# Loading the attention stacks of a group with six loads instead of seven, parts interleaved row by row

## The reference

```
q = layernorm(x) @ Wq;  k, v = split(ctx @ Wkv)        # 32 heads of 16
q, k = rope(q, pos), rope(k, pos)
x = x + softmax(q k^T / 4) v @ Wout + bout
h = gelu(bitlinear(layernorm(x), w_fc))                # 512 -> 2048
x = x + bitlinear(h, w_proj)                           # 2048 -> 512
```

## Time and profile before

| | us |
|---|---|
| median of 3 runs | 797.15 |
| the runs | 799.24, 793.47, 797.15 |
| the profiled execution | 797.79 |
| its span | 795.9 |
| busy: TensorE | 768.5 (97%) |
| busy: VectorE | 674.4 (85%) |
| busy: ScalarE | 456.1 (57%) |
| busy: GpSimd | 341.0 (43%) |

### The profile page before, as it was taken

The page is one execution under the profiler, slowest core; times in us unless marked ns, Lnnn a source line. Parts: engine busy times, 40 slices in busy tenths (PEclk is TensorE's granted clock), DMA queues, the critical chain, the costliest instruction groups (busy, mean ns, idle before and its releaser), DMA issues.

```text
span 795.9 us, 11662 instructions
## 1 busy us (share of the span) xinstructions
PE 768.5 (97%) x3812; PEld 331.6 (42%) x3812; DVE 674.4 (85%) x945; ACT 456.1 (57%) x811; POOL 341.0 (43%) x445
## 2 busy tenths in 40 slices
PE   4899999799999999999999999999999999999998
PEld 3688877233333222323322222244444444444443
DVE  7788998688888888888888888269999999898895
ACT  5677776477777777767777777734322333223430
POOL 4688777743454455445445544623222121110001
PEclk9999999699999999999999999999999999999999
DMA  8488897535577769796887996326456654555545
GB/s 288 127 216 241 256 254 184 129 109 137 147 141 152 154 158 142 152 171 149 146 155 180 171 176 137 82 57 137 107 110 144 132 106 93 108 117 87 112 87 137
DMA packets 178861, 117.22 MB, mean 147 GB/s; under 512 B 119746, under 2 KB 150514, under 8 KB 178802
## 3 DMA queue, kind: packets, MB, share of 16 engines
q1 hardware_dynamic: 178802, 116.49, 65.7%
HBM read 64.50 MB, written 25.43 MB: 113 GB/s over the span
## 4 chain that ended last, share of the span: by engine, by line
PE 86%; DMA 6%; DVE 3%; SPq 2%; POOL 1%; issue 1%; ACT 1%; POOLq 0%; ACTq 0%
PE banks L967 14%; PE banks L952 14%; PE banks L706 13%; PE banks L692 12%; PE banks L281 11%; PE banks L667 11%; PE banks L938 7%; DMA stack_words<-max_rows 4%; DMA max_rows<-max_parts 2%; PE banks L310 2%; SPq L584 1%; PE banks L678 1%; DVE maxima L740 1%; DMA attn_words<-in_x_dram 1%; ACT probs_words L760 1%
## 5 line engine op out<-in xcount | busy, mean ns | idle before, releaser
L760 ACT ACTIVATE probs_words<-banks 128x512 f32<-128x512 f32 x512 | 272.1, 598 | 101.7 <-PE banks L692 101.0
L740 DVE TENSOR_REDUCE maxima<-banks 128x2 f32<-128x1024 f32 x240 | 283.4, 1216 | 45.6 <-PE banks L667 45.5
L692 PE MATMUL banks<-stack_words 98*128 98x512 bf16 x512 | 175.4, 386 | 4.8 <-DMA stack_words<-max_rows 3.4
L667 PE MATMUL banks<-stack_words 96*128 96x512 bf16 x480 | 144.9, 383 | 0.0
L706 PE MATMUL banks<-probs_words,late_words 128*32 128x512 f32 x1024 | 137.3, 608 | 0.7
L952 PE MATMUL banks<-ternary_words,late_words 128*128 128x512 f16 x512 | 113.1, 380 | 0.0
L967 PE MATMUL banks<-ternary_words,stack_words 128*128 128x512 f16 x512 | 112.9, 380 | 0.0
L1130 ACT ACTIVATE probs_words<-probs_words,h_moments 128x2048 f32<-128x2048 f32 (+1 forms) x17 | 32.2, 1901 | 135.4 <-DVE h_moments L1027 135.4
L692 PEld LDWEIGHTS banks<-stack_words 98*128 98x128 bf16 x512 | 39.8, 98 | 150.0 <-ACT probs_words L760 109.9
L771 POOL TENSOR_SCALAR neg_max<-maxima 128x16 f32<-128x16 f32 x32 | 8.3, 258 | 163.0 <-DVE maxima L740 161.2
L967 PEld LDWEIGHTS banks<-ternary_words,stack_words 128*128 128x128 f16 x512 | 49.9, 98 | 64.4 <-issue 6.6
(11 more groups left out here) (139 smaller groups left out, 962.5 us busy)
## 6 DMA issues: line engine op xcount, KB each, us to landing
o_rows<-late_words SPq DMA_DIRECT2D x32, 256.0 KB, 3.3
k_parts<-ternary_words SPq DMA_DIRECT2D x48, 128.0 KB, 3.2
q_parts<-ternary_words SPq DMA_DIRECT2D x48, 128.0 KB, 2.5
stack_words<-q_parts SPq DMA_DIRECT2D x32, 192.0 KB, 3.1
stack_words<-k_parts SPq DMA_DIRECT2D x96, 64.0 KB, 2.7
stack_words<-k_parts SPq DMA_DIRECT2D x32, 192.0 KB, 2.7
attn_words<-in_x_dram SPq DMA_DIRECT2D x16, 256.0 KB, 4.4
probs_words<-in_L_ffn_w_fc_dram SPq DMA_DIRECT2D x16, 256.0 KB, 3.7
```

Of the source, the lines that this page charges most:

```text
L667: mm = self.nc.tensor.matmul(self.score_slot[j % 2][:, i], self.mem.q_stack[0:STACK, slot, head, c * P:(c + 1) * P], self.mem.k_stack[0:ST ...
L692: self.nc.tensor.matmul(self.st_bank[(g * 16 + k) % self.ST_BANKS], self.mem.k_stack[0:STACK + 2, slot, head, c * P:(c + 1) * P], self.mem ...
L740: dve.tensor_reduce(self.maxima[:, g % 2, 2 * j:2 * j + 2], self.score_slot[j % 2], AX.X, ALU.max).then_inc(self.scores_read, 1)
L760: act.activation(self.probs[:, c, head, :], self.st_bank[(g * 16 + k) % self.ST_BANKS], ACT.Exp, scale=1 / math.sqrt(HEAD)).then_inc(self. ...
```

## The change

`load_stacks` views the parts as (value) x (part) x (head, column): 16 rows in the outer dimension, the parts within. A load of several parts writes partition after partition in that order, so a stack's block of 48 partitions holds value 0 of parts 0, 1, 2, then value 1 of parts 0, 1, 2, and so on. `k_stack` gets in each such block one part of k repeated: part 0 three times, part 1 twice, part 2 once, by a source view that repeats the part. The pairs are the same six: q's parts 0, 1, 2 with k's part 0, q's 0, 1 with k's 1, and q's 0 with k's 2. There are six loads, q and k in turn, of 192, 192, 128, 128, 64 and 64 KB, 768 KB as before. Their place in SP's list is the same. `STACK_LOADS` follows.

```diff
-STACK_LOADS = DMA * 7
+STACK_LOADS = DMA * 6
...
-        for stack_sb, where, runs in (
-            (mem.q_stack, mem.q_parts, ((0, 0, 3), (3, 0, 2), (5, 0, 1))),
-            (mem.k_stack, mem.k_parts, ((0, 1, 1), (1, 0, 1), (2, 0, 1), (3, 0, 3))),
-        ):
-            src = where[g].rearrange("t (d h) c -> (t d) (h c)", h=GH)
-            for to, part, count in runs:
-                sp.dma_start(stack_sb[to * HEAD:(to + count) * HEAD, slot].rearrange("p h c -> p (h c)"),
-                             src[part * HEAD:(part + count) * HEAD]).then_inc(self.stacks_loaded[slot], DMA)
+        q_rows, k_rows = [where[g].rearrange("t (d h) c -> d t (h c)", h=GH) for where in (mem.q_parts, mem.k_parts)]
+        for part, to, count in ((0, 0, 3), (1, 3, 2), (2, 5, 1)):
+            at = slice(to * HEAD, (to + count) * HEAD)
+            sp.dma_start(mem.q_stack[at, slot].rearrange("p h c -> p (h c)"), q_rows[:, 0:count]
+                         ).then_inc(self.stacks_loaded[slot], DMA)
+            sp.dma_start(mem.k_stack[at, slot].rearrange("p h c -> p (h c)"),
+                         k_rows[:, part:part + 1].to_broadcast([HEAD, count, GH * SEQ])
+                         ).then_inc(self.stacks_loaded[slot], DMA)
```

## The result

The changed kernel takes 798.76 us in the median (796.05 to 805.09, 20 runs), the kernel before 797.28 us (793.47 to 799.24, 20 runs). The ratio is 1.0036 with a 95% interval of 1.0021 to 1.0050: 0.36%, 2.9 us, slower.

A forecast was written before the change was run, and what follows sets the result against it. TensorE was taken as the bound, its loop stalls hanging on the row maxima's load. Issue +0.5 and transfer 0 on the median 797.15 gave 797.7 us, set at 797.4 for a small gain; range near 791.5 to near 802.

The forecast's parts named there:

- the slack that I had read: Attention loop: in a group without a backlog the row maxima's load L596 has at least 1.2 us to spare.
- The bound: Attention loop: of TensorE's 3.44 us idle, 3.4 us in 6 waits is for the 8 KB row maxima load, L596.
- The issue term: SP's issue of the stack loads: six take 3.43 us, 0.17 longer than seven before.
- The transfer term: DMA engines carrying the 768 KB of stacks: taken as 0, with 1.3 us either way as the ends.
- What it costs: Attention loop: only the 6 groups with a TensorE wait pay 0.17 us each, +1.0 us, half taken: +0.5 us.
- The rule on joining small transfers: DMA queue: one load fewer would give 0.6 us a group, up to 3.4 us over six late groups; sum had 0.
- A: Rival: one load fewer on SP and in the queue ends the 6 maxima waits, 793.7 us, half 795.4; chance 0.24.
- B: Rival: the new source form is slow to carry, queue 1.3 us a group later, 807 us; chance 0.11.
- C: Rival: loads leave SP as seven would, with the same durations, 797.15 us within the runs' spread; chance 0.02.

The follow-up runs named there:

- runs with one plain side: Changed kernel with only q's, or only k's, three loads as plain consecutive rows (wrong pairing of parts): 1.0037, 799.30 us with plain q; 1.0022, 798.29 us with plain k.
- six plain loads: Order and number of the change's loads, but all of plain consecutive rows (other scores), against the kernel before: 0.9993, 796.16 us.
- nine loads: Kernel before with q's and k's loads of 48 rows each cut into 32 and 16, same rows and bytes: 1.0093, 803.77 us.

## Why the prediction was right or wrong

The class was right (within 1%), the sign too, and the time lies in the range; the size was not. I had +0.25 us on the median; the ratio says +2.9. That the class came out right is in part luck: two terms were too small, and the slack that I had read hid most of it. Of the signs that I named, six issues in a group with a sum of 3.61 us, L596 at 4.88, a period of 11.35 us in most groups and no wait of the score product came true; TensorE's wait of at most 5 us (it is 6.3 in this profile) and the queue's share near 51% (55 to 63%) did not. Step by step:

**The bound.** Right. The only stall that hangs on the loads is TensorE's wait for L596. It grew from 3.4 to 6.3 us, in a profile 5.8 us above its kernel's median. In the runs above it went roughly with the lateness of that load: 0.9 us with L596 at 4.10, 1.1 and 3.4 with 4.57, 3.1 to 3.5 with 4.67 to 5.03, 7.0 with 5.49.

**The issue term.** Right in sign, mis-sized: 0.17 us predicted, 4.88 - 4.58 = 0.30 measured. I took 0.575 us from the row of a source with a repeated dimension, and the loads with several parts took 0.58 to 0.63. What I missed is that q's load of 16 rows, plain in my sum with 0.42, took 0.58 too. The runs with one plain side show the cause: the issue behind a load of this form is also longer.

**The transfer term.** This is the step that failed. I took 0, with 1.3 us at the far end. Measured is an arrival 1.2 us later, of which 0.9 us is landing (2.7 to 3.6 us). The reason I gave, 64 KB and 192 KB landing in the same 2.7 us, was weak, since the profile does not measure loads of one semaphore apart, and it did not carry over to another order and number of loads. It was not the source form, as I had thought possible, but the rest: q and k in turn give about 0.6 us of arrival, six loads in place of seven 0.3 (7.7 us, with the issue 0.47 us shorter), the form 0.3 by its issue.

**What it costs.** I let only the 6 groups that had a wait pay, once each, and half of that. Who pays was right: calm groups take the whole 1.2 us out of their slack and wait for nothing (8 KB at 8.0 to 8.7 us, wanted at 8.99). What each late group pays was too low. In groups with a late transpose the 8 KB land 0.35 us later in the middle case (9.14 to 9.49), and 7 groups wait in place of 6. Seven to nine groups at 0.35 us are 2.5 to 3.2 us by my estimate, the size of the 2.9 measured.

**The rule on joining small transfers** ("DMA: Bandwidth & Descriptors" of the Trainium skill, section Rules for kernel authors), by which I had estimated 0.6 us a group for one load fewer, did not show in the time: with six plain loads it stayed (0.9993; the interval reaches 2.0 us down, not 3.4), and the bytes came later, not sooner. TensorE's waits did fall in that profile, from 3.4 to 0.9 us. The table of that page of the Trainium skill, from which the 0.6 us came, is of transfers that GpSimd issues to 128 partitions, which these are not.

**The rivals.** A did not occur: no wait went away. B had the mechanism, bytes that arrive late and a point at 1.2 us a group, and the wrong cause and price; the arrival stood just at that point, and the time 2.9 us up and not 10. C is ruled out by the timeline.

## What to carry to other kernels

Look for the small transfer that the critical engine waits for, and count what is issued and what is queued ahead of it: here 8 KB behind 768 KB. Fewer DMA issues are not less issue time when their sources get another dimension; and the price of lateness is paid where the small transfer is already late for another reason: 1.2 us of delay made no calm group wait, and 0.35 us in the late ones is about the size of the whole loss. Issuing the small transfer ahead of the last of the big ones gave more (0.3%) than any form of the big ones, as long as these still landed in time; moving big loads ahead of the small one's own producer gave nothing or harm.

## What the runs showed of the hardware

In the profiled run of the changed kernel at 804.57 us TensorE waited 2.36 us at 161.39 (and 1.94 us at 478.23), and then ran slow, which the profiled run of before does not do from 158 us on. Both runs have a slow stretch ahead of that, at the start of the loop, and in the changed kernel it ended earlier: from 150 to 158 us the clock was granted at 0.97, before at 0.61. L592 of group 1 starts at nearly the same time in both, 155.41 and 155.80. So TensorE, further on in the changed kernel, came to the maxima of group 1 before they were there. The lines are before, then after; the granted clock is third from the right:

```profile
150.00:158.00 8.00, 8.00 (x31) 1.99 (x29) 4.74 (x5) 4.53 (x9) 7.66 (x6) 0.61 0.36 56
150.00:158.00 8.00, 8.00 (x46) 2.22 (x44) 6.51 (x7) 5.74 (x11) 7.66 (x7) 0.97 0.53 57
```

The windows around the wait, of the changed kernel:

```profile
158.00:160.00 2.00, 1.04 (x8) 0.31 (x4) 1.52 (x2) 1.09 (x2) 0.05 (x1) 1.00 0.01 1
160.00:162.00 2.00, 0.61 (x2) 0.33 (x3) 0.30 (x1) 0.00 (x0) 1.36 (x4) 0.69 0.38 127
162.00:164.00 2.00, 2.00 (x8) 0.35 (x9) 1.11 (x1) 1.19 (x2) 2.00 (x2) 0.50 0.43 91
164.00:166.00 2.00, 2.00 (x11) 0.37 (x4) 0.81 (x2) 0.28 (x1) 1.92 (x3) 0.50 0.66 174
166.00:168.00 2.00, 2.00 (x7) 0.61 (x5) 0.99 (x1) 1.38 (x3) 0.05 (x1) 0.60 1.02 197
168.00:170.00 2.00, 2.00 (x13) 0.56 (x13) 1.36 (x2) 1.06 (x3) 0.00 (x0) 1.00 0.71 184
```

At half clock (1.2 GHz in place of 2.4) from 162 to past 166 us, eight matmuls of L706 took 1.94 us in place of 1.06. A wait of 1.58 us at 430.73 left the clock at 1.00, as did all waits of before in the loop, at most 1.1 us. Other kernels above show such falls too. With nine loads it came behind this wait, and the window from 456 to 458 us has 0.50:

```profile
454.37 0.39 PE L692 MATMUL banks<-stack_words 98*128 98x512 bf16 x1 [1.66 <-DMA stack_words<-max_rows]
456.00:458.00 2.00, 2.00 (x8) 0.46 (x5) 1.15 (x2) 0.68 (x3) 2.00 (x2) 0.50 0.44 113
```

With q ahead of the transpose it came with waits of 3.33 us (seven loads, 475.28) and 1.84 us (six, 161.13), but not with 1.82 and 1.73 us at 449 in the same two. So a wait for a late load can cost more than its own length, and its length alone does not tell whether it will. Two runs of the changed kernel's twenty lie above 804 us, and none of before lies above 799.3. Both have a mean granted clock of 0.985, where most have 0.987 to 0.991; a run of 800.46 us has 0.985 too, so the clock is a part of it, not all.
